# First attention: queries and keys turned into separate buffers, queries with the head innermost, one score product per head

## The reference

```python
# B=16 blocks of 128 tokens, each with a context of 128 rows of 256; H=16 heads of D=128
q = (layernorm(x) @ Wq).reshape(B, 128, H, D)
k = (ctx @ Wk).reshape(B, 128, H, D)
v = (ctx @ Wv).reshape(B, 128, H, D)
q, k = rmsnorm(q, gq), rmsnorm(k, gk)
attn = softmax(einsum('bqhd,bkhd->bhqk', q, k) / sqrt(D))
x = x + einsum('bhqk,bkhd->bqhd', attn, v).reshape(B, 128, H * D) @ Wo
```

## Time and profile before

| | |
|---|---|
| median of 3 runs | 1988.04 us (1986.86 to 1989.33) |
| profiled execution, span of its instructions | 1985.1 us |
| TensorE products / weight loads, busy | 1935.9 us (98%) / 1562.9 us (79%) |
| DVE / ACT / POOL, busy | 1315.2 us (66%) / 742.2 us (37%) / 564.5 us (28%) |
| sends of turned blocks (L259) | 64 of 512 KB, 2.9 us from issue to landing |
| loads of turned blocks (L264) | 64 of 512 KB, 4.3 us from issue to landing |
| DMA packets, all | 126294, of which 72688 under 2 KB |

### The profile page before, as it was taken

How to read it: one execution, slowest core, us unless ns; L and a number is a source line. 1 busy time by engine, 2 the same in 40 slices (tenths; PEclk the granted TensorE clock), 3 DMA queues, 4 the chain that set the end, 5 groups by cost and what they waited for, 6 DMA issues and landing times. The chain is left out here.

```text
span 1985.1 us, 35876 instructions
## 1 busy us (share of the span) xinstructions
PE 1935.9 (98%) x13552; PEld 1562.9 (79%) x13552; DVE 1315.2 (66%) x2493; ACT 742.2 (37%) x2275; POOL 564.5 (28%) x705
## 2 busy tenths in 40 slices
PE   6999999899999999999999899999999999999999
PEld 4888888778888878888888677777688888888887
DVE  6656655665555654343345599988868878888786
ACT  5555455654555543111122344444433222122211
POOL 3322222322223425310121343433310222322231
PEclk9999999999999999999999899999999999999999
DMA  6632333433444433020122100000112546555654
GB/s 233 221 103 90 99 114 108 165 112 117 137 148 143 144 107 128 27 80 32 32 69 93 63 28 18 21 23 19 54 54 70 191 154 210 192 192 167 201 163 160
DMA packets 126294, 222.39 MB, mean 112 GB/s; under 512 B 17392, under 2 KB 72688, under 8 KB 126192
## 3 DMA queue, kind: packets, MB, share of 16 engines
q1 hardware_dynamic: 102480, 134.01, 20.5%
q0 software_dynamic: 23712, 87.04, 13.2%
HBM read 170.16 MB, written 50.86 MB: 111 GB/s over the span
## 5 line engine op out<-in xcount | busy, mean ns | idle before, releaser
L2385 POOL DMA_INDIRECT m_ring<-in_table,m_row x128 | 127.3, 994 | 370.0 <-DVE l_x_all L2498 264.1
L48 PE MATMUL four_banks<-l_yT_hi,m_hi 128*128 128x512 f32 x512 | 199.4, 389 | 0.0
L48 PE MATMUL four_banks<-l_yT_lo,m_hi 128*128 128x512 f32 x512 | 199.2, 389 | 0.0
L1147 DVE TENSOR_SCALAR f_relu<-bank,f_b 128x512 f32<-128x512 f32 x64 | 48.0, 750 | 166.3 <-ACT f_h_hi L1090 166.3
L529 ACT ACTIVATE prob<-four_banks,mx,rms 128x128 f32<-128x128 f32 x256 | 114.0, 454 | 114.3 <-DVE mx L667 114.3
L328 POOL TENSOR_TENSOR rms<-ssq,constants 128x4 f32<-128x4 f32 x128 | 34.9, 273 | 391.9 <-ACT junk_k L518 237.9
L1090 ACT ACTIVATE f_h_hi<-bank,f_b 128x512 fp32r<-128x512 f32 x64 | 44.2, 690 | 255.6 <-PE bank L48 255.6
L331 POOL TENSOR_TENSOR rms<-rms,constants 128x4 f32<-128x4 f32 x128 | 130.1, 1016 | 10.0
L48 PEld LDWEIGHTS four_banks<-l_yT_hi,m_hi 128*128 128x128 f32 x512 | 96.1, 188 | 20.1 <-issue 0.2
L48 PEld LDWEIGHTS four_banks<-l_yT_lo,m_hi 128*128 128x128 f32 x512 | 96.1, 188 | 20.0
L2362 ACT ACTIVATE m_act_of<-m_dot,l_ln_y 128x2 f32<-128x2 f32 x64 | 19.0, 297 | 238.6 <-DVE m_junk L2488 238.6
(11 more groups left out here) (316 smaller groups left out, 5410.2 us busy)
## 6 DMA issues: line engine op xcount, KB each, us to landing
turned<-blocks SPq DMA_DIRECT2D x64, 512.0 KB, 2.9
qkT<-turned SPq DMA_DIRECT2D x64, 512.0 KB, 4.3
f_stage<-in_w POOLq DMA_DIRECT2D x14, 512.0 KB, 4.6
f_x_in<-x SPq DMA_DIRECT2D x18, 256.0 KB, 3.5
ctx_in<-in_ctxT SPq DMA_DIRECT2D x32, 128.0 KB, 2.6
x_in<-in_x SPq DMA_DIRECT2D x16, 256.0 KB, 2.7
x<-xres SPq DMA_DIRECT2D x16, 256.0 KB, 2.1
x<-l_x_all SPq DMA_DIRECT2D x16, 256.0 KB
```

What stands on the lines that cost most here:

```text
L48: mm = pe.matmul(out, st, mv, start=first and n == 0, stop=last and n == len(terms) - 1)
L1147: dve.tensor_scalar(relu[m % 2][:], bank[HB[m % 2]][:], b12[:, layer, m:m + 1], 0.0, ALU.add, ALU.max).then_inc(S["relu_ready"], 1)
L2385: pool.indirect_dma_start(ring[slot][:], None, table, bass.IndirectOffsetOnAxis(ap=row[:, tile_of(g), k:k + 1], axis=0)).then_inc(S[f"got{ ...
```

## The change

Queries and keys get tiles of their own. `blocks[g]` keeps its size, but has the queries in one half and the keys in the other. The queries' transposed blocks are written with the head innermost, so that four heads alternate in memory, and the keys' as before, with the head outside. In DRAM, `turned` is split in the same way. The loads become two DMAs per half of a step, one for queries into `qT[g]` and one for keys into `kT[g]`, each of half the bytes; TensorE waits for both (32 instead of 16 on the semaphore). The score of a head becomes one product: its stationary operand is the head's 128 queries, read with a step of 4 elements, and its moving operand the 128 keys as before.

```diff
-        oT0_hi ... blocks0 4 blocks1 4 qkT0 4 ...
+        oT0_hi ... blocks0 4 blocks1 4 qT0 2 kT0 2 ...
-    blocks = [sb(f"blocks{g}", [P, 4, 2 * G, 32], F32) for g in range(2)]
-    qkT = [sb(f"qkT{g}", [P, 4, 2 * G, 32], F32) for g in range(2)]
+    blocks = [sb(f"blocks{g}", [P, 2, 4, G * 32], F32) for g in range(2)]
+    qT = [sb(f"qT{g}", [P, 4, 32, G], F32) for g in range(2)]
+    kT = [sb(f"kT{g}", [P, 4, G, 32], F32) for g in range(2)]
...
         def send(s, g):
             sp.wait_ge(*at(f"k_blocks{g}", s))
             sp.wait_ge(*at(f"q_blocks{g}", s))
-            sp.dma_start(turned[g].rearrange("p (j b) r -> (p j) (b r)", b=4), blocks[g][:].rearrange("p b h i -> p (b h i)")
+            sp.dma_start(turned[g].rearrange("t p (j b) r -> (p j) t (b r)", b=4), blocks[g][:].rearrange("p t b r -> p t (b r)")
                          ).then_inc(S[f"qk_stored{g}"], 16)
 
         def bring(s, g):
             sp.wait_ge(S[f"qk_stored{g}"], 16 * (s + 1))
-            sp.dma_start(qkT[g][:].rearrange("d p h i -> d p (h i)"), turned[g].rearrange("p d r -> d p r")
+            sp.dma_start(qT[g][:].rearrange("d p i h -> d p (i h)"), turned[g][0].rearrange("p d r -> d p r")
+                         ).then_inc(S[f"qk_loaded{g}"], 16)
+            sp.dma_start(kT[g][:].rearrange("d p h i -> d p (h i)"), turned[g][1].rearrange("p d r -> d p r")
                          ).then_inc(S[f"qk_loaded{g}"], 16)
...
         def score(s, g):
-            pe.wait_ge(S[f"qk_loaded{g}"], 16 * (s + 1))
+            pe.wait_ge(S[f"qk_loaded{g}"], 32 * (s + 1))
...
+            rows = qT[g][:].rearrange("d p i h -> d (p i) h")
             for j in range(G):
-                for p in range(4):
-                    out = bank[(1, 3)[g]][32 * p:32 * (p + 1), j * P:(j + 1) * P].rearrange("q (p i) -> q p i", p=4)
-                    mm = pe.matmul(out, qkT[g][:, p, j, :], qkT[g][:, :, G + j, :], start=True, stop=True)
+                out = bank[(1, 3)[g]][:, j * P:(j + 1) * P].rearrange("q (p i) -> q p i", p=4)
+                mm = pe.matmul(out, rows[:, :, j], kT[g][:, :, j, :], start=True, stop=True)
...
-            dve.transpose(blocks[g][:, :, 0:G, :], blocks_of(bank[(7, 3)[g]][:])).then_inc(S[f"q_blocks{g}"], 1)
+            dve.transpose(blocks[g][:, 0].rearrange("p b (i h) -> p b h i", h=G), blocks_of(bank[(7, 3)[g]][:])).then_inc(S[f"q_blocks{g}"], 1)
...
-            dve.transpose(blocks[g][:, :, G:2 * G, :], blocks_of(k_sb[:])).then_inc(S[f"k_blocks{g}"], 1)
+            dve.transpose(blocks[g][:, 1].rearrange("p b (h i) -> p b h i", h=G), blocks_of(k_sb[:])).then_inc(S[f"k_blocks{g}"], 1)
...
-    turned = nc.dram_tensor("turned", (2, 4, P, 256), F32).ap()
+    turned = nc.dram_tensor("turned", (2, 2, 4, P, P), F32).ap()
```

More of the change, by code:

```diff
@@ L101, in l0_attention @@
         wv1_hi 4 wv1_lo 4 wo0_hi 8 wo0_lo 8 wo1_hi 8 wo1_lo 8 stage0 8 stage1 8 stage2 8 xres 32 x_in 2 xn 2 xT_hi 2 xT_lo 2
-        ctx_in 1 ctx_hi 1 ctx_lo 1 k_sb 2 v_sb0 2 v_sb1 2 blocks0 4 blocks1 4 qkT0 4 prob0 2 prob1 2 pT_sb0 2 pT_sb1 2
+        ctx_in 1 ctx_hi 1 ctx_lo 1 k_sb 2 v_sb0 2 v_sb1 2 blocks0 4 blocks1 4 qT0 2 kT0 2 prob0 2 prob1 2 pT_sb0 2 pT_sb1 2
         oT0_hi 2 oT0_lo 2 oT1_hi 2 oT1_lo 2 gains .5 junk_q 1""")
@@ L105, in l0_attention @@
         rms1 .09375 constants .09375 mx0 .03125 mx1 .03125 den0 .03125 den1 .03125""")
-    spots |= spots_of(200, "qkT1 4")
-    spots["gk"] = spots["qkT0"]
+    spots |= spots_of(200, "qT1 2 kT1 2")
+    spots["gk"] = spots["kT0"]
     spots["junk_k"] = spots["k_sb"]
```

## The result

The changed kernel takes 2046.93 us (median of 4 runs, 2044.04 to 2048.55) against 1988.68 us before (median of 4 runs as well): ratio 1.0293, 95% interval 1.0278 to 1.0307. The change costs 58 us. The profiled execution spans 2044.9 us against 1985.1.

What follows compares the result with a forecast made beforehand. The prediction took a 22.06 us serial loop through half 0's load as the bound. Transfer +0.5 and score -0.05 gave +0.45 us over 30 steps, +13.5; with 2.9 from span to median, 2001.5 us, 8-in-10 range 1989 to 2062.

Steps and rivals of the forecast that it cites:

- the second rival: Strided weight loads and query transposes both run at half rate: +2.35 us per step, 2058 us, chance 0.24.
- Strided weight reads: Query weights of the scores: forecast no cost, the lower end; upper end +0.86 us per score, half 0's in the loop.
- Transposes: DVE's strided query writes: forecast no cost; upper end, at half rate, +0.52 us for each of two, both in the loop.
- Transfer: Loads and send in smaller rows: +0.2 to +0.9 us per step, taken as +0.5, landing 4.8 us instead of 4.3.
- the third rival: Two loads in flight overlap better, landing moves under 0.13 us a step: no measurable change, 1984 to 1992 us, chance 0.09.
- The loop: Serial chain in the first attention from half 0's load through score, DVE, ACT and send to the next load: 22.06 us.
- TensorE's own work is 21.71 us.: TensorE's length per step, 22.06 less a 0.35 us wait for half 0's load: nearly as long as the loop, not last.
- the fourth rival: Faster: half 0's load lands earlier or the wide score saves more in the loop; -9 us, 1979 us, chance 0.11.
- Half 1's score "isn't in the loop": Its burst is over by 259.1, before DVE comes to its maxima at 259.73, so TensorE's saved 0.31 us isn't in the loop.
- rivals 1 and 2: Half-rate weight loads alone, 1.31 us per step, 2027 us, chance 0.20; with half-rate transposes too, 2.35, 2058 us, 0.24.
- The number of steps: The loop binds in about 30 of 32 steps, excluding the prologue and weight-exchange steps: 30 x 0.45 = +13.5 us.
- TensorE's longer wait: Before each first score, TensorE's wait grows from 0.35 to about 1.2 us.

Runs made afterwards that it cites:

- e3: The changed kernel with dense transpose writes and dense weight reads (neighbouring elements, mixed-up rows), split transfer and wide products kept: 1990.45 us.
- e4: The kernel before with separate query and key tiles, the split send and two loads, layout dense, still 16 narrow products per half: 1992.75 us.
- e7: The changed kernel with dense transposes and the step of four in one half's weight reads only: half 1 alone 2002.37 us, half 0 alone 2017.33.
- e5: The kernel before, with SyncE issuing the load of half 0 ahead of the send of half 1: 2006.43 us.
- e9: The kernel before, with half 0's load issued after half 0's send and half 1's send issued by ACT on its own queue: 2006.62 us.
- e11: e4 with half 0's keys loaded ahead of half 1's send and half 0's queries after it: 1994.96 us.
- e12: The kernel before, with the copy of half 1's turned probabilities moved from DVE to ACT: 1988.16 us.
- e14: The kernel before with e12's edit and, for half 1 alone, wide products at a step of two, queries loaded in 256-byte pieces: 1986.46 us.
- e13: e3 and e12 in one, the changed kernel with dense writes and reads and ACT's copy: 1972.79 us.

## Why the prediction was right or wrong

The direction and the range held (2046.9 us, in 1989 to 2062); the forecast of 2001.5 us did not, nor its own range up to 2016.5. What happened is the second rival (2058 us): both strided operations slowed.

- *Strided weight reads.* The step that failed: "I take the lower end, as the nearer row shows no cost at all." It put both strided terms at nothing. The runs show +0.97 us per step in the loop for the weight reads of half 0's score (e3 against the changed kernel) and +0.68 for the two transposes. The upper end, +0.86 us per score, had 107 ns more per weight load (128 x 0.84), measured 137. The table's +0.85 is this 0.97 less the 0.12 that the wide product saves, where the prediction had -0.05: two small errors that nearly cancel. The row chosen as the nearest, a step of two, is nearest in number and lies on the other side of the cause: at two elements each 16 bytes are hit twice, at four once. The prediction said so itself in its next paragraph, and kept the lower end. The sentence of the Trainium skill that spoke against the change (SBUF — State Buffer, Door 1) held for the second access to a line, and the traces agree, with 329 ns against 192; a price for each move to a new line, which the prediction quotes with it, doesn't show at a step of two (196 ns). The rival that it stood beside was given 0.24 only.
- *Transposes.* The same choice, and less than the half rate of the upper end: +0.52 us each, measured +0.38 (1.053 against 0.674), or 0.34 in the loop. Rival 2's 2.35 us per step become the measured 1.75 with 0.36 less for the two transposes and 0.49 less for the transfer, and with 0.04 more for half 0's score, 0.19 for half 1's and 0.02 elsewhere. Its 2058 us came within 11 us of the time with terms that were too high by up to 0.5 us a step, and without the 5.6 us of the exchange of weights, which no term had; that it came so near is in part luck.
- *Transfer.* Forecast +0.5 us per step, measured -0.15 from the issue to the score and +0.16 from the transpose over the send to the next issue: nothing together, with some 0.2 us of spare time ahead of the score used up. e4 puts it at 3 us for the whole stage, e3 at about none. The row time was right: while only the small rows of half 1's loads move in the changed kernel, 924 packets take 90.0% of 16 engines over 1.7 us, 26.5 ns each:

```profile
q1 hardware_dynamic: 924, 0.46, 90.0%
```

  The send was near its upper bound, 3.2 us from issue to landing against 2.9 for half 1. But of the 4.3 us landing only some 1.5 is row time, and that the loads landed no later because two in flight overlap, as the third rival argued, wasn't tested.
- *The loop.* Its links are right, and they carried the result: in the changed kernel they add up to the period with no other one. That it already set the step before the change isn't so: TensorE came last there, at 22.06 us, and the loop was some 0.1 to 0.2 us shorter. Half 0's score counts in full, half 1's for less than half (e7).
- *"TensorE's own work is 21.71 us."* Wrong by the whole 0.35 us, an idle time taken as a wait because the profile named the load as its releaser. It had no effect on the forecast's sign, but the fourth rival's "up to 0.7 us" and the gain expected of e5, e9, e11 and e12 hung on it.
- *Half 1's score "isn't in the loop".* It ended 0.6 us before DVE came; the strided reads used that up and 0.19 us more. The sums of rivals 1 and 2 had left that out.
- *The number of steps.* Between the last loads of the 32 steps lie 31 intervals. 28 grew by 1.79 us on the mean, 50 us; the exchange of weights between the passes, two intervals, took 56.5 us for 50.9, 5.6 more; the first took 0.4 more. That is 56 of the 57 us. The strides account for little of the exchange's part, as e3 without them still has 4.2 us more than the kernel before. In the changed kernel TensorE waits 3.7 us for the keys there, and the granted clock is 0.50, its lower level, from 398.4 to 405.2 us. The prediction's 30 steps of one size were near enough.
- *TensorE's longer wait.* Forecast 1.2 us before each first score, measured 0.73: the loop grew by more, but TensorE grew as well, by an estimate to 21.44 + 2 x 0.85 = 23.14 us of the 23.81.

## What to carry to other kernels

When a layout change makes an operand strided, count how often each 16 bytes of SBUF are hit, not how large the step is: one product in place of four saved TensorE 0.31 us per burst, and the layout with its elements four apart, read by TensorE and written by DVE, cost 3% of the whole kernel, while two apart cost nothing. For DVE's writes only steps of 1, 2 and 4 were measured. A wait of a few tenths whose releaser is a landing may be the engine's own gap, so look for the same gap where nothing is awaited. And where two bounds have nearly the same length, test a change to one only together with a change to the other. The time from a load's landing to its use, step by step, and whether the period varies, tell which of the two comes last.

## What the runs showed that I had not expected

- The cost of strided weight reads is graded: +4, +69 and +137 ns for 128 columns at steps of 2, 3 and 4 elements of 4 bytes.
- The DVE transpose, which writes 512 elements, pays for its output's step as well: 0.674 us at one and two elements, 1.053 at four.
- A send of 512 KB issued 0.3 to 0.5 us after a load of 512 KB in rows of 1 KB lands after 5.2 us (same queue) or 5.6 us (ACT's queue), and 2.9 us when it is issued first. In rows of 2 KB it lands after 3.6 us behind a load of 256 KB in rows of 512 bytes, and 3.2 us when it is issued first. Why the second queue doesn't help stays open.
- Bursts of 16 narrow products cost TensorE 0.31 us more than bursts of 4 wide ones that read neighbouring elements, though the weight loads of a wide burst span no less time (0.81 us narrow, 0.97 wide in e3): its period went from 22.06 us (e12) to 21.79 with one wide burst (e14) and 21.45 with two (e13).
- The exchange of weights takes 50.9 and 50.6 us in the two kernels whose granted clock stays at its upper level there (before, e9), 51.0 to 55.1 where it is at the lower one for some 3.4 us, and 52.5 to 56.5 where it is for some 6.8 us (the changed kernel has the 56.5). The clock goes with it but doesn't fix it.
